# A two-layer decoder on one core: the next sequence's u projection ranked below the running tail

## The reference, cut to what matters

```python
x = ln(x + L0_attn(x))        # Mamba block, 1024 channels, 16 states, then a SwiGLU feed-forward of 1408
x = ln(x + L0_xattn(ctx, x))  # second Mamba on ctx, 512 channels, 16 states; x gates its output
x = ln(x + L0_ffn(x))         # 8 experts, top 2, and a shared SwiGLU of 704
x = ln(x + L1_attn(x))        # attention inside groups of 4 tokens and a memory
x = ln(x + L1_xattn(x, ctx))  # attention map from ctx, applied to x
x = ln(x + L1_ffn(x))         # top 8 of 64, biases gathered
```

## Time and profile before

| | us |
|---|---|
| runs shown, median (lowest to highest) | 3427.14 (3421.89 to 3434.63) |
| profiled execution | 3423.53 |
| its span | 3421.8 |
| DVE busy | 2614.8 (76%) |
| PE busy | 2456.9 (72%) |
| ACT busy | 1118.4 (33%) |
| POOL busy | 965.1 (28%) |

### The profile page before, as it was taken

How to read it: one execution, slowest core, us unless ns; L and a number is a source line. 1 busy time by engine, 2 the same in 40 slices (tenths; PEclk the granted TensorE clock), 3 DMA queues, 4 the chain that set the end, 5 groups by cost and what they waited for, 6 DMA issues and landing times. The chain is left out here.

```text
span 3421.8 us, 20262 instructions
## 1 busy us (share of the span) xinstructions
PE 2456.9 (72%) x6316; PEld 1167.1 (34%) x6316; DVE 2614.8 (76%) x2060; ACT 1118.4 (33%) x1754; POOL 965.1 (28%) x279
## 2 busy tenths in 40 slices
PE   5676121489878765689887865699797856979875
PEld 1233000134334432333443422333343433444433
DVE  2896989899799889998998978994998973122023
ACT  2432232343333534334324433334324411111121
POOL 0132434323244252323242441330352440000000
PEclk7775555699989986799989976799899877989996
DMA  2155000011126640112135630112136620215740
GB/s 78 32 156 150 0 7 0 19 62 63 56 74 203 202 125 6 49 57 65 59 103 186 200 109 0 49 63 65 52 105 198 190 91 33 72 52 171 250 134 12
DMA packets 151195, 307.87 MB, mean 90 GB/s; under 512 B 29808, under 2 KB 47216, under 8 KB 150000
## 3 DMA queue, kind: packets, MB, share of 16 engines
q1 hardware_dynamic: 130864, 261.41, 24.8%
q10 hardware_dynamic: 15104, 28.38, 2.3%
q0 software_dynamic: 5120, 16.78, 1.4%
HBM read 278.21 MB, written 43.78 MB: 94 GB/s over the span
## 5 line engine op out<-in xcount | busy, mean ns | idle before, releaser
L1659 POOL TENSOR_TENSOR ya<-ya,hb 128x2048 f32<-128x2048 f32 x180 | 823.4, 4575 | 1156.7 <-DVE hb L1367 1142.9
L1367 DVE TENSOR_TENSOR_SCAN hb<-da,hb 128x2048 f32<-128x2048 f32 x192 | 867.2, 4517 | 1.4
L1006 ACT ACTIVATE da<-dl,pk 128x511 f32<-128x511 f32 x768 | 489.6, 709 | 644.7 <-DVE hb L1367 575.9
L1278 DVE TENSOR_TENSOR hb<-du,ps 128x2048 f32<-128x2048 f32 x192 | 435.8, 2270 | 36.3 <-PE ps L674 26.9
L1375 DVE TENSOR_TENSOR hb<-hb,ps 128x2048 f32<-128x2048 f32 x192 | 437.4, 2278 | 0.9
L674 PE MATMUL ps<-bct,sel 64*128 64x512 f32 x192 | 114.4, 596 | 369.6 <-DVE hb L1278 363.3
L703 PE MATMUL ps<-V,ring 128*128 128x512 f32 x512 | 245.9, 634 | 16.1 <-DVE yg L1319 8.6
L664 PE MATMUL ps<-ring,hid 128*128 128x512 f32 x544 | 248.7, 613 | 8.3 <-ACT X L1157 7.0
L853 PE MATMUL ps<-ring,hid 128*128 128x352 f32 x480 | 196.6, 492 | 36.1 <-DMA ring<-egu 33.5
L674 PEld LDWEIGHTS ps<-bct,sel 64*128 64x128 f32 x192 | 41.9, 218 | 503.4 <-DVE hb L1278 409.0
L780 PE MATMUL ps<-bct,sel 64*128 64x512 f32 x192 | 104.8, 546 | 123.7 <-DVE hb L1375 123.2
(11 more groups left out here) (240 smaller groups left out, 3395.4 us busy)
## 6 DMA issues: line engine op xcount, KB each, us to landing
ring<-egu SPq DMA_DIRECT2D x240, 352.0 KB, 3.5
ring<-in_w_edn SPq DMA_DIRECT2D x72, 512.0 KB, 5.0
ring<-in_w_fgu SPq DMA_DIRECT2D x44, 512.0 KB, 3.7
ring<-in_w_in SPq DMA_DIRECT2D x32, 512.0 KB, 3.6
hid<-xrows SPq DMA_DIRECT2D x60, 256.0 KB, 3.6
yrows<-X ACTq DMA_DIRECT2D x60, 256.0 KB, 4.4
ring<-in_w_egu SPq DMA_DIRECT2D x24, 512.0 KB, 3.4
ring<-in_w_edn SPq DMA_DIRECT2D x60, 192.0 KB, 4.5
```

The costliest lines, as they stand in the source:

```text
L1006: i = act.activation(dav(n % 2)[:, k, 1:], dl[:, k, 1:], ACT.Exp, scale=Aneg[:, (4 * (u % 3 - 1) if u % 3 else UC) + k, m:m + 1])
L1278: dve.tensor_tensor(hbv(m % NHB), du[:, :, :], wide(ps[:, 5, :], 4), ALU.mult).then_inc(s["dbu"], 1)
L1367: dve.tensor_tensor_scan(hb[:, h, :], da[:, b % 2, :], hb[:, h, :], 0.0, ALU.mult, ALU.add)\
L1659: pool.tensor_tensor(ya[:, :, :], ya[:, :, :], hbv(m % NHB), ALU.add).then_inc(s["acc"], 1)
```

## The change

Three edits; no instruction of the computation is added or taken away.

1. The tasks `hx_load`, `p_sq`, `p_nrm`, `p_mm` 0 to 7, `p_ev`, `p_th`, `p_bc`, `p_bt`, `p_bb`, `p_bs` go from rank 20 to rank 32, on all engines. The tail keeps 30, the gate half 35.
2. In the plan, PE's task of a unit's first state may not start before 4.4 us ahead of the end of that state's DVE task (which the plan costs at 6.75 us: `dbu` and the scan).
3. The first two "rows" items move in SP's list from behind the last shared-expert load to ahead of the first routed block's loads.

```diff
-            put(10, ("sa", n, 0), "pe", 0.65, back, (("dt_c", q, 0), "pe"))
+            put(10, ("sa", n, 0), "pe", 0.65, back, (("dt_c", q, 0), "pe"), (("sa", n, 0), "dve", -4.4) if n == first else None)
...
-        put(20, ("hx_load", b, 0), "act", 0.1, (("t_sq", b - 1, 0), "pool") if b else None,
+        put(32, ("hx_load", b, 0), "act", 0.1, (("t_sq", b - 1, 0), "pool") if b else None,
             (("t_rs", b - 1, 0), "dve") if b else None)
         for k in range(KC):
-            chain(20, ("p_sq", b, k), [("act", 0.6), ("pe", 0.9)], (("hx_load", b, 0), "act", 6),
+            chain(32, ("p_sq", b, k), [("act", 0.6), ("pe", 0.9)], (("hx_load", b, 0), "act", 6),
                   (("p_sq", b, k - 2), "pe") if k >= 2 else None, (("c_bc", b, 0), "dve"))
-        at = chain(20, ("p_nrm", b, 0), [("act", 2.7), ("dve", 2.9)], (("p_sq", b, KC - 1), "pe"))
+        at = chain(32, ("p_nrm", b, 0), [("act", 2.7), ("dve", 2.9)], (("p_sq", b, KC - 1), "pe"))
         for n in range(UC):
-            put(20, ("p_mm", b, n), "pe", 3.6, at, (("p_ev", b, n - 2), "dve") if n >= 2 else None,
+            put(32, ("p_mm", b, n), "pe", 3.6, at, (("p_ev", b, n - 2), "dve") if n >= 2 else None,
                 (("p_mm", b, n - 1), "pe") if n else None)
...
                 elif t == "exp_mm":
                     n.append((w_egu[i],) + of("gu", b, FA + i + 1))
-                    if i == SHARED - 1:
-                        n.append(("rows", b, 0))
-                        n.append(("rows", b, 1))
                 elif t == "bg":
                     j, k = divmod(i, 4)
+                    if i == 0:
+                        n += [("rows", b, 0), ("rows", b, 1)]
                     if k == 0:
                         n.append(("pick", b, j))
```

More of the change, by code:

```diff
@@ L147, in plan @@
                 (("p_mm", b, n - 1), "pe") if n else None)
-            chain(20, ("p_ev", b, n), [("act", 0.75), ("dve", 2.6)], (("p_mm", b, n), "pe"),
+            chain(32, ("p_ev", b, n), [("act", 0.75), ("dve", 2.6)], (("p_mm", b, n), "pe"),
                   (("p_ev", b, n - 1), "act") if n else None)
-            chain(20, ("p_th", b, n), [("act", 0.6), ("dve", 0.7)], (("p_ev", b, n), "dve"))
-        put(20, ("p_bc", b, 0), "pe", 3.6, (("p_th", b, UC - 1), "dve"))
-        at = chain(20, ("p_bc", b, 1), [("pe", 3.6), ("act", 0.6)], (("p_bc", b, 0), "pe"))
@@ L153, in plan @@
[L153 to L156, removed]
+            chain(32, ("p_th", b, n), [("act", 0.6), ("dve", 0.7)], (("p_ev", b, n), "dve"))
+        put(32, ("p_bc", b, 0), "pe", 3.6, (("p_th", b, UC - 1), "dve"))
@@ L157, in plan @@
+        at = chain(32, ("p_bc", b, 1), [("pe", 3.6), ("act", 0.6)], (("p_bc", b, 0), "pe"))
+        at = chain(32, ("p_bt", b, 0), [("pe", 0.9), ("act", 2.7), ("dve", 0.75)], at)
+        put(32, ("p_bb", b, 0), "pe", 3.6, at)
+        at = chain(32, ("p_bb", b, 1), [("pe", 3.6), ("act", 0.6)], (("p_bb", b, 0), "pe"), (("dt_mm", 3 * b, 3), "pe"))
+        at = chain(32, ("p_bs", b, 0), [("pe", 0.9), ("act", 2.7), ("dve", 2.2)], at)
         for n in range(UC, 2 * UC):
```

## The result

The changed kernel takes 3504.9 us (median of 4 runs, 3500.7 to 3506.6) against 3426.0 for the kernel before: a ratio of 1.0233, 95% interval 1.0215 to 1.0251. It is 79 us slower, above the range of the prediction (3335 to 3480). Every line number from 557 on is one lower than before, because edit 3 is one line shorter: L1366 is the scan, L702 a u or gate-half product, L828 and L835 the two products of a chunk of feed-forward or expert.

A forecast was written before the change was run, and what follows sets the result against it. It took the chain of tails, not the scans, to bound the kernel: 3423.5 + 7 (ranks) − 15 (hint) = 3415.5, stated as 3418 because the profiled execution lay 3.6 below the median; range 3335 to 3480.

The forecast's parts named there:

- What bounds the kernel: Whole span: a tail, not the scans, is what the next tail waits for; a change pays if it shortens tails.
- Feed-forward alone: Tail 2: feed-forward without the projection, from +48, takes 119 us plus 8 for scan rows and the rest, ending at +175.
- u ready: Tail 2, after the feed-forward: squares, eight u products, convolutions and tanh done at +214 us from the start of `mix`.
- The rows ahead of the expert: Tail 2: B and C rows ready at +245, shared expert before gate half, first scan of unit 10 at +285.
- The bare way from one to the other: From the end of `route_a` to the first block's transpose, no longer hidden behind the expert: 44 us.
- Per tail: First routed transpose 15 us sooner in tail 0, 10 sooner in tail 1, 8 later in tail 2: 17 gained.
- The lost scan-free end: End of tail 2, from the last block to the last statistics: later scans cover some 112 us, costing 24 more than before.
- The hint: PE's first row at unit starts: idle waits on `dbu` removed, 15 us gained in all, between 0 and 35.
- Edit 3: SP's sorted-row loads moved: costs nothing while no slot is awaited in between, at worst 11 us over three tails.
- Rival 1: First scan of the x Mamba comes late and scans take over the tails' ends: slower, 3472 us, chance 0.23.
- Rival 3: Bare projection chain on PE's slow clock, u products 6.5 us instead of 3.5: slower, 3490 us, chance 0.08.
- Rival 2: Gate half gets ahead of the shared expert, which covers the routing wait: faster, 3342 or 3346 us, chance 0.21.

The follow-up runs named there:

- rows_29: The changed kernel with the B and C row tasks (`p_bc`, `p_bt`, `p_bb`, `p_bs`) at rank 29, above the tail; 3437.6 us, ratio 1.0043.
- late_scans: The kernel before with the hint, step sizes of unit 3b+1 held back in the plan until the running tail's `route_a` is done; 3410.6 us, ratio 0.9968.
- late_gate: The kernel before with the hint and moved row loads, gate half held back in the plan until the shared expert is done; 3486.1 us, ratio 1.0187.
- no_hint: The changed kernel without the later placing of PE's first row of a unit; 3537.4 us, ratio 1.0326.
- rows_gate_29: The changed kernel with the B and C rows and the gate half at rank 29, above the shared expert, u products still at 32; 3397.0 us, ratio 0.9919.
- by_sequence: The changed kernel with rows and gate half at 29 for projections of sequences 0 to 2, ranks of before for sequence 3; 3386.8 us, ratio 0.9888.

## Why the prediction was wrong

The forecast was "no change", 3418, and 3505 was measured. By its own steps, in tail 2:

- **What bounds the kernel:** right. Tails follow each other, and in the changed kernel all three times the statistics (L1600) released `mix`, no unit's end.
- **Feed-forward alone:** forecast to end at +175, measured +183. The scan rows and the last DVE wait were worth 16, not 8 (119 + 16 behind +48). That makes everything behind it 8 late.
- **u ready:** forecast +214, measured +227. The extra 5 are one wait of 8.8 us for DVE, which had the norm behind `res_t` and the end of unit 9 before the convolution.
- **The rows ahead of the expert: this is the step that failed.** The order between expert and gate half was as I said, but I let the B and C rows finish first, at +245, and they came at +303. The rows have rank 32 and the expert has 30; I had compared the expert with the gate half's 35 only. My own sum shows the gap: it starts the expert at +236 and still has the rows done at +245, although L729 needs PE in between. `gate` was done at +238 and its norm at +253, so the expert started right behind the B and C product and L729, one short matmul, waited behind all twelve products. The scans then began at +340, where I had +285. The gate half ran by itself from +302 to +350, 48 us instead of 31, because `dt_mm` and `dt_c` of unit 10, which need the rows, fell into the same stretch. `route_a` ended at +356 (forecast +317), and the transpose came at +400 (forecast +361). The bare way from one to the other was 44, as forecast.
- **What that step is worth:** rows_29 puts only the rows back ahead of the expert and measures 3437.6, so 67 of the miss of 87 us. The other 20 lie in the sizes of other terms.
- **Per tail:** I had the first transpose 15 and 10 sooner in tails 0 and 1 and 8 later in tail 2. It is 9, 22 and 47 later: 78 lost where I had 17 gained, an error of 95. In tail 2 the error is 39: 20 were there before the expert began (+256 instead of +236), 17 came in the gate half, 2 in the rest. Over the whole span 8 were to be gained and 83 were lost. These 91 are the 95 at the transposes, less 17 that the rest of the tails lost less than I had forecast, 8 in the lone tail, and 5 because the start gave 10 where I had 15 for the hint.
- **The lost scan-free end:** forecast 24, and right in size against the kernel before: from the first transpose to the statistics tail 2 takes 374 us instead of 354 (late_scans 378). But with a routing as late and scans early, in late_gate, the same part takes 311. Tail 1 gained 17 in it, which I had not forecast.
- **The hint:** forecast 15, measured 25 by itself and 32 within the change.
- **Edit 3:** nothing with the ranks of before, as forecast.
- **Rival 1** had the side right and some of the size (3472), but its mechanism, `mix` waiting for a unit's end, ended no tail of the changed kernel. It stood 6, 6 and 15 us behind, and it does decide in no_hint and in tail 2 of late_scans. A forecast near it would have been right by luck. **Rival 3,** the slow clock, was no cause by itself: the six u products in a row take 3.8 us each (23.06 for six), not 6.5; single products behind an idle take 5.7 and 6.4, and the clock of 0.58 in the bare stretch comes with PE's idleness there. The 0.84 for the whole tails fits the waits; no run takes the clock apart from them. **Rival 2** was an ordering that one more rank would have given: rows_gate_29 measures it at 3397, where I had priced 3346. I took the time won at the first transpose for time won at the end, and the ctx convolutions and the routed blocks took most of it back.

What stays open: how the loss of tails 0 and 1 divides between the late routing and the scans that ended 6 us behind it; why the lone tail takes 536 to 539 us in the changed kernel, no_hint, rows_29, rows_gate_29 and by_sequence and 528 to 534 in the others, slow and quick kernels alike; and why the routed blocks of late_gate's tail 1 took 20 us more than with the hint alone, with a DMA share of 0.59 instead of 0.65 and a clock of 0.88 instead of 0.94. No run took that apart.

## What to carry to other kernels

Ranks in a list scheduler are not about one pair of tasks. When a chain moves below something, every link of it moves below it, the 1 us links as well, and a short link that a long chain waits for is what ends up behind the block of work. Before moving a filler, look for what waits for it at the far end (here the routing, through the gate half), and ask whether the work that used to hide that wait has just been spent in front of it. A gain or a loss of one stage is to be followed to the stage that ends the chain: 39 us at the first routed block were 11 at the end. And delays need not add up: apart, the late routing and the late scans cost tail 2 some 10 and 33 us, together 81.

## What was not expected of the hardware

In the kernel before some DVE scans were held up while POOL was adding. Here are a tiny one of the routing and a large one, on DVE and then on POOL:

```profile
979.95 4.28 DVE L1519 TENSOR_TENSOR_SCAN hid<-unit,hid 128x8 f32<-128x8 f32 x1
...
2521.61 9.00 DVE L1367 TENSOR_TENSOR_SCAN hb<-da,hb 128x2048 f32<-128x2048 f32 x1
```

```profile
979.68 4.51 POOL L1659 TENSOR_TENSOR ya<-ya,hb 128x2048 f32<-128x2048 f32 x1 [12.26 <-DVE hb L1367]
...
2521.78 4.53 POOL L1659 TENSOR_TENSOR ya<-ya,hb 128x2048 f32<-128x2048 f32 x1
```

The tiny scan (L1519) takes 0.17 us elsewhere and took 4.28 here, until POOL's addition was over. The large one (L1367) takes 4.42 elsewhere, and 9.00 is this and nearly all of POOL's 4.53. The Trainium skill, "SBUF — State Buffer" ("SBUF: two separate sides"), says that DVE and POOL share a pair of ports, and that of a DVE operation with two inputs in SBUF and a POOL operation that reads SBUF the one that starts first holds them for its whole instruction while the other blocks. The tiny scan agrees: POOL had started 0.27 us before it. Of the large one the records show the wait but not the order, since its own start is recorded 0.17 us ahead of POOL's. Among the large scans this happened seldom: the mean of the 192 is 4.52 us before and 4.48 after, so it is no part of the difference.
